# Group loop of a graph rotation: a pass now inverts, moves and applies its own group, the V chain stands ahead of the loop, and SyncE loads the edges

## What is computed

```python
x = x + gnn(xn, edge_weight, src, dst) + mix(xn)
x = x + ffn(layernorm(x))

# gnn: a product of plane rotations, in the order of the edges; mat starts as the identity (256x256)
ri, rj = mat[i], mat[j]
mat = mat.at[i].set(c * ri - s * rj)
mat = mat.at[j].set(s * ri + c * rj)
# ... return x @ mat.T
# mix: sm = softmax(keys, over the rows); lam = sm.T @ value; bn = batch norm of lam; return query @ bn
# ffn: 8 experts, the two best of each row, gelu between two products
```

## Time and profile before

| | |
|---|---|
| median of three runs | 741.78 us |
| the profiled execution's own time | 743.47 us |
| its span (first to last instruction) | 741.6 us |
| busy TensorE, VectorE, ScalarE, GpSimd | 87%, 64%, 60%, 53% |

### The profile page before, as it was taken

The page is one execution under the profiler, slowest core; times in us unless marked ns, Lnnn a source line. Parts: engine busy times, 40 slices in busy tenths (PEclk is TensorE's granted clock), DMA queues, the critical chain, the costliest instruction groups (busy, mean ns, idle before and its releaser), DMA issues.

```text
span 741.6 us, 18150 instructions
## 1 busy us (share of the span) xinstructions
PE 646.9 (87%) x4083; PEld 552.9 (75%) x4084; DVE 477.8 (64%) x1883; ACT 443.4 (60%) x1226; POOL 394.1 (53%) x541
## 2 busy tenths in 40 slices
PE   6789899754498999229999999899989999999996
PEld 5467667522487777129998999899979999999996
DVE  4996666699867688624454444444457777777775
ACT  6776566477033399616665666566656666666663
POOL 7203877145532267733776776432246665656654
PEclk7889999955599999759999999999999999999999
DMA  7830012246410267622443333322223333333332
GB/s 202 263 88 10 21 31 26 43 127 219 138 34 2 60 197 242 220 89 88 144 132 126 118 121 122 93 65 69 63 70 103 107 99 107 105 101 95 106 95 70
DMA packets 60591, 78.10 MB, mean 105 GB/s; under 512 B 15688, under 2 KB 49350, under 8 KB 60288
## 3 DMA queue, kind: packets, MB, share of 16 engines
q1 hardware_dynamic: 44989, 41.67, 20.5%
q0 software_dynamic: 14976, 35.38, 14.5%
q10 hardware_dynamic: 576, 0.54, 0.2%
HBM read 47.53 MB, written 31.53 MB: 107 GB/s over the span
## 4 chain that ended last, share of the span: by engine, by line
PE 66%; DVE 12%; issue 7%; DMA 5%; POOL 5%; ACT 2%; SPq 1%; DVEq 1%; POOLq 0%; ACTq 0%
PE banks L2679 21%; PE banks L2689 20%; PE banks L2305 6%; PE banks L2631 5%; PE banks L2284 4%; POOL send_d L900 3%; PE banks L2670 3%; DMA R<-send_d 2%; DVE R L1743 1%; DMA out_dram<-R,dest_now 1%; DMA R<-in_x_dram 1%; PE banks L2295 1%; DVE R L1758 1%; DVE R L1322 1%; PE banks L2523 1%
## 5 line engine op out<-in xcount | busy, mean ns | idle before, releaser
L2679 PE MATMUL banks<-R 128*128 128x128 f32 x1696 | 209.0, 277 | 2.6 <-ACT R L1271 2.6
L2679 PEld LDWEIGHTS banks<-R 128*128 128x128 f32 x1696 | 199.7, 193 | 3.2 <-ACT R L1271 3.1
L2689 PE MATMUL banks<-R 128*128 x848 | 200.4, 379 | 0.0
L1284 ACT ACTIVATE R<-banks,b1c 128x128 f32<-128x128 f32 x424 | 142.9, 364 | 51.4 <-PE banks L2679 51.3
L2689 PEld LDWEIGHTS banks<-R 128*128 128x128 f32 x848 | 153.1, 190 | 16.4
L1271 ACT ACTIVATE R<-banks,bet_c,gam_c 128x128 f32<-128x128 f32 x212 | 85.4, 453 | 115.0 <-PE banks L2670 112.5
L2192 DVE COPY R<-R 128x1024 f32 x106 | 74.5, 703 | 77.9 <-PE banks L2679 61.8
L900 POOL DMA_INDIRECT send_d<-R,slot_all x98 | 98.4, 1004 | 44.5 <-issue 39.1
L913 POOL DMA_INDIRECT first_d<-R,dest_now x54 | 61.2, 1134 | 91.4 <-DVE R L2197 77.7
L922 POOL DMA_INDIRECT R<-first_d,get_now x52 | 54.0, 1038 | 49.1 <-DVE get_now L2174 46.0
L913 POOL DMA_INDIRECT out_dram<-R,dest_now x52 | 63.7, 1225 | 29.6 <-issue 26.3
(11 more groups left out here) (561 smaller groups left out, 960.3 us busy)
## 6 DMA issues: line engine op xcount, KB each, us to landing
R<-send_d SPq DMA_DIRECT2D x106, 131.0 KB
...
send_d<-R,slot_all POOLq DMA_INDIRECT x98
...
```

Source lines behind the costliest of these rows:

```text
L1284: last = nc.scalar.activation(hT[b][:, c, :], bank[2 + 2 * b + c // 2][:, (c % 2) * P:(c % 2 + 1) * P], ACT.Gelu, bias=b1c[:, bass.ds(e, 1 ...
L2679: last = mm(bank[2 + 2 * b + c // 2][:, (c % 2) * P:(c % 2 + 1) * P], w1c[b][:, kb, c * P:(c + 1) * P], xmT[b][:, kb * P:(kb + 1) * P], st ...
L2689: last = mm(bank[6 + b][:, 0:D], hT[b][:, c, :], w2s[:, bass.ds(e, 1), c, :].rearrange("p a h -> p (a h)"), start=(c == 0), stop=(c == H / ...
```

## The change

It has four parts. (1) A pass of the loop runs the six levels first and then transforms and applies its own group; no empty group, no application behind the loop. (2) The V chain, the router's sums and the split of the added row stand ahead of the loop, parts of them among the placing of the events. (3) Behind the loop Mrot is first added to the base (L1972 before) and the sum is turned; one product (L2592 before), its copy and one sum over the matrix are gone, and the row sums come with the copy out of the PSUM bank. (4) SyncE loads the edges behind `load_x(1)`, `load_x(2)` waits for nothing, and on VectorE `count_rest` stands ahead of the first `mix_step`.

The loads, GpSimd's list, and VectorE's first steps:

```diff
-                if i == 2:
-                    sp.wait_ge(S["edges"], 96)
                 sp.dma_start(x_all[:, c:c + 8, :], xg_src[:, c:c + 8, :]).then_inc(S[f"xld{i}"], 16)
...
+            load_x(1)
+            for dstt, s in ((hi_raw.bitcast(I32), src), (hj_raw.bitcast(I32), dst), (h_theta, edge_weight)):
+                sp.dma_start(dstt, s[0:HP * HL].rearrange("(p l) -> p l", p=HP)).then_inc(S["edges_h"], 16)
+            for dstt, s in ((i_raw, src), (j_raw, dst), (theta, edge_weight)):
+                for into, out_of in zip(parts_of(dstt), parts_of(s.rearrange("(p l) -> p l", p=EP))):
+                    sp.dma_start(into, out_of).then_inc(S["edges"], 16)
+            for i in range(2, FULL // 8):
                 load_x(i)
...
                 link(nc.gpsimd.memset(padd[:, c:c + 1], -1.0))
-            for dstt, s in ((hi_raw.bitcast(I32), src), (hj_raw.bitcast(I32), dst), (h_theta, edge_weight)):
-                nc.gpsimd.dma_start(dstt, s[0:HP * HL].rearrange("(p l) -> p l", p=HP)).then_inc(S["edges_h"], 16)
-            for dstt, s in ((i_raw, src), (j_raw, dst), (theta, edge_weight)):
...
-            pool.wait_ge(S["ngroups"], 1)
-            n = pool.value_load(n_groups_i[0:1, 0:1], min_val=1, max_val=4 * NE)
-            with loop(pool, 0, n) as k:
...
-            pool.wait_ge(S["recs_in"], n * (16 * G) + 3 * 16 * G)
+            pool.wait_ge(S["recs_in"], 3 * 16 * G)
...
+            pool.wait_ge(S["ngroups"], 1)
+            n = pool.value_load(n_groups_i[0:1, 0:1], min_val=1, max_val=4 * NE)
+            with loop(pool, 0, n) as k:
+                fields(k + 2)
+                gather_steps(k + 3)
+
+
+            pool.wait_ge(S["recs_in"], n * (16 * G) + 3 * 16 * G)
...
             row_stats("xld1", 8, 16).then_inc(S["xstats_ok"], 1)
+            count_rest()
             mix_step(0)
             scales(3)
-            count_rest()
             count_head()
```

ScalarE's copies and the batch norm ahead of the loop, and VectorE's part of it (`tl` and `own` make VectorE wait for the instruction itself):

```diff
+                if c == 9:
+                    turned_back(PT, P_TURNED)
                 if c == 24:
                     pair_angles(0)
             pair_angles(1)
+            turned_back(wqT, WQ_TURNED)
+            table_of(ACT.Sqrt)
+            act.wait_ge(S["lamstats_ok"], 1)
+            nc.scalar.activation(small[:, 4:6], mvl[:, :, 1], ACT.Sqrt, bias=eps).then_inc(S["act"], 1)
+            act.wait_ge(S["lamstats_ok"], 2)
+            for kb in range(KB):
+                last = nc.scalar.activation(bn[:, kb, :], lam[:, kb, :], ACT.Identity, bias=small[:, 10 + kb:11 + kb], scale=small[:, 8 + kb:9 + kb])
+            last.then_inc(S["bn_ok"], 1)
 
...
+                dve.wait_ge(S["pe"], VALUES)
+                nc.vector.memset(addrow[:, D + NX:DC], 0.0)
+                for kb in range(KB):
+                    last = STT(lam[:, kb, :], bank[5][:, kb * D:(kb + 1) * D], rsum[:, kb:kb + 1], bvB[:, :], ALU.mult, ALU.add)
+                tl(last)
+                for kb in range(KB):
+                    last = nc.vector.bn_stats(lamstats[:, kb, :], lam[:, kb, :])
+                tl(last)
+                for kb in range(KB):
+                    last = nc.vector.bn_aggr(mvl[:, kb, :], lamstats[:, kb, :])
+                last.then_inc(S["lamstats_ok"], 1)
...
+                dve.wait_ge(S["edge_pe"], U_A)
+                tl(own_keys(0))
+                tl(own_values(0))
+                tl(own_sums(0))
+                dve.wait_ge(S["act"], LAM_ROOTS)
+                nc.vector.reciprocal(bn_scale, small[:, 4:6])
+                dve.wait_ge(S["edge_pe"], U_B)
+                tl(own_keys(1))
+                TT(bn_scale, bn_scale, bng_c[:, :], ALU.mult)
+                tl(own_values(1))
+                STT(bn_shift, mvl[:, :, 0], -1.0, bn_scale, ALU.mult, ALU.mult)
+                tl(own_sums(1))
...
             dve.wait_ge(S["empty_group"], 1)
+            dve.wait_ge(S["pe"], ROW_ADDED)
+            nc.vector.tensor_copy(add_c[:, :], bank[6][:, AT_ADD:AT_ADD + KB])
+            TT(brB[:, :], bank[6][:, AT_SUMS + NX:AT_SUMS + 2 * NX], brB[:, :], ALU.add)
+            nc.vector.tensor_copy(addrow[:, 0:D], bank[6][:, 0:D])
+            for kb in range(KB):
+                last = STT(comb[:, kb, D + NX:AVG], bank[6][:, AT_SUMS:AT_SUMS + NX], -1.0 / D, wrg[:, kb, :], ALU.mult, ALU.add)
+            last.then_inc(S["setup_own"], 1)
             first_guess(0)
+            dve.wait_ge(S["setup_own"], 1)
+            own(nc.vector.tensor_reduce(addrow[:, AVG:AVG + 1], addrow[:, 0:D], AX_X, ALU.add))
+            TS(addrow[:, AVG:AVG + 1], addrow[:, AVG:AVG + 1], 1.0 / D, None, ALU.mult)
             find_last(0)
+            dve.wait_ge(S["pe"], LOGIT_ADDED)
+            nc.vector.tensor_copy(addrow[:, D:D + NX], bank[6][:, AT_LOGITS:AT_LOGITS + NX]).then_inc(S["addrow_ok"], 1)
```

VectorE's loop, and what stands behind it:

```diff
                 other_rows(k)
+                factor(k, 1)
                 find_hits(k1, (0, 1))
-                factor(k, 1)
-                apply_m(k, 0)
+                factor(k, 2)
                 find_hits(k1, HALVES[1])
-                factor(k, 2)
+                factor(k, 3)
                 find_latest(k1)
-                apply_m(k, 1)
-                factor(k, 3)
+                factor(k, 4)
+                rows_read(k)
+                factor(k, 5)
+                kept(k)
                 mark_latest(k1)
-                apply_m(k, 2)
-                factor(k, 4)
                 own_reads(k1)
                 other_part(k1)
                 build_L(k1)
-                factor(k, 5)
-                rows_read(k)
+                apply_m(k, 0)
+                first_guess(k1)
                 find_last(k1)
...
-
+            own(last)
+            own(TT(Mrot[:, :, D - 1], Mrot[:, :, D - 1], flush[:, 1, :], ALU.add))
             dve.wait_ge(S["recs_in"], n * (16 * G) + 3 * 16 * G)
             dve.wait_ge(S["flds_ready"], n + 2)
             dve.wait_ge(S["Y_ready"], n + 1)
-            dve.wait_ge(S["pe"], 7)
+            dve.wait_ge(S["pe"], BASE)
             TT(turned0, bank[1].rearrange("p (a b) -> p a b", a=KB), Mrot[:, :, :], ALU.add).then_inc(S["combT_ok"], 1)
             dve.wait_ge(S["comb_pe"], 1)
-            dve.wait_ge(S["comb_moved"], 1)
-            TT(comb[:, :, 0:D], comb[:, :, 0:D], TB.rearrange("p (a b) -> p a b", a=KB), ALU.add).then_inc(S["comb_dve"], 1)
+            for kb in range(KB):
+                last = STT(comb[:, kb, 0:D], TB[:, kb * D:(kb + 1) * D], 1.0, zrow[:, 0:D], ALU.mult, ALU.add, accum_out=csum[:, kb:kb + 1])
+            last.then_inc(S["comb_dve"], 1)
             dve.wait_ge(S["comb_dve"], 1)
-            nc.vector.tensor_reduce(csum[:, :], comb[:, :, 0:D], AX_X, ALU.add).then_inc(S["comb_dve"], 1)
-            dve.wait_ge(S["comb_dve"], 2)
```

TensorE:

```diff
                     spread_rows(g + 2)
+            values()
             pe.wait_ge(S["pair_dve"], FULL_ROWS)
             mm(bank[6][:, 0:KB], ones[:, :], bad[:, 5:7], start=True, stop=True).then_inc(S["edge_pe"], 1)
...
-            for _ in range(14):
+            router_sums()
+            for _ in range(6):
                 mm(bank[6][:, 0:P], ident[:, :], ident[:, :], start=True, stop=True)
+            added_row()
...
+            added_logits()
 
             n = pe.value_load(n_groups_i[0:1, 0:1], min_val=1, max_val=4 * NE)
 
             with loop(pe, 0, n) as k:
-                transform(k)
                 residual(k, 0)
                 spread_targets(k + 1)
                 better(k, 0)
-                apply_v(k, 0)
                 residual(k, 1)
-                apply_m(k, 0)
                 better(k, 1)
                 residual(k, 2)
-                apply_v(k, 1)
                 better(k, 2)
-                apply_m(k, 1)
                 residual(k, 3)
-                apply_v(k, 2)
                 better(k, 3)
-                apply_m(k, 2)
                 residual(k, 4)
                 better(k, 4)
                 residual(k, 5)
                 count_writes(k)
+                better(k, 5)
+                transform(k)
+                apply_v(k, 0)
+                apply_m(k, 0)
                 count_later(k + 1)
                 turn_L(k + 1)
-                better(k, 5)
-            transform(n)
-            pe.wait_ge(S["wload"], 16 * 10)
-            pe.wait_ge(S["pn_ok"], 1)
...
+                apply_m(k, 2)
+            base_rows(0)
+            base_rows(1).then_inc(S["pe"], 1)
+            for _ in range(3):
+                mm(bank[0][:, 0:P], ident[:, :], ident[:, :], start=True, stop=True)
+            pe.wait_ge(S["combT_ok"], 1)
             for a in range(KB):
                 for b in range(KB):
-                    last = tr(TB[:, b * D + a * P:b * D + (a + 1) * P], Mrot[:, a, b * P:(b + 1) * P], ident[:, :])
+                    last = tr(TB[:, b * D + a * P:b * D + (a + 1) * P], turned0[:, a, b * P:(b + 1) * P], ident[:, :])
             last.then_inc(S["comb_pe"], 1)
-            pe.wait_ge(S["combT_ok"], 1)
             for ib in range(KB):
                 for a in range(KB):
```

(2 more changed lines are left out.)

241 lines of the change are left out of this document (96 added, 145 removed).

## The result

The changed kernel took 737.4 us (median of 20 runs, 731.64 to 744.54), the kernel before 742.55 in runs beside it (20 runs, 738.78 to 745.75). The ratio is 0.9934, 95% interval 0.9912 to 0.9955: 3.3 to 6.5 us faster, where 11.2 were forecast. Every ratio in this document is to the kernel before in runs beside it on the same chip, and leaves out runs more than 1.5 per cent above the fastest of their kernel (here 743.48 and 744.54).

A forecast was written before the change was run, and what follows sets the result against it. Part three was taken as a chain of short steps, TensorE busy 34.34 of 39.00 us, its empty-group work waste. Terms -3.8 + 0.5 - 2.4 - 1.85 - 3.65 = -11.2 us gave 730.6 us on the median, range 727 to 733.5 (0.66).

The forecast's parts named there:

- A: Part one, loads and first steps: load_x(1) lands earlier and the weighted-sum products start sooner and run shorter, -3.8 us.
- B: Part two and the start of the loop, up to the first residual: added and removed work sum to +0.5 us.
- Rival 2: TensorE enters the levels at half clock after fewer identity products, some 3 us more, 733.6 us; chance 0.12.
- The prediction's own sign against itself: The forecast is wrong if PEclk, the granted clock, is below 1 in the loop.
- C: The six levels: without the 128x256 products between residual and better, 14.8 us against 17.16, -2.4 us.
- D: From transform to the last application: V chain's products and sums gone, 11.75 us against 13.6, -1.85 us.
- E: Behind the last application: first sum comes 4.45 us later against 8.1, -3.65 us.
- late gather: Within E, VectorE's sum behind the loop waits for GpSimd's last gathered records; without it 0.9 us less.
- Behind 247.00 nothing is changed, and its start moves as a whole: From the first sum on, experts included, the kernel only starts earlier and takes as long as before: 0 us.
- Rival 3: Half the gain is given back later, by a wait of the routing for GpSimd or a load: 736 us; chance 0.06.
- Rival 4: Granted clock falls to half in the whole loop without the removed products: +15.3 us, +4.1 net, 745.9 us; chance 0.04.

The follow-up runs named there:

- loads_only: The kernel before with part (4) alone (edges on SyncE behind load_x(1), no wait in load_x(2), count_rest earlier): 739.82 us, ratio 0.9978.
- fill_pool: The changed kernel with identity products ahead of the loop, at its entrance and in the levels' waits, and GpSimd's loop ahead of the split again: 738.23 us, ratio 0.9931.
- fill_early: The changed kernel with 8 and 3 more identity products in TensorE's two waits around the product of the composites: ratio 0.9913 to the kernel before.
- ident14: The changed kernel with 14 identity products in place of 6 ahead of the added row: ratio 1.0033 to the kernel before.
- loop_only: The changed kernel with part (4), the loads, undone: 740.32 us, ratio 0.9961 to the kernel before.

## Why the prediction was wrong

The mechanisms were named rightly, and two sizes and one sentence were not.

- **A, mis-sized (-3.8 forecast, -2.7 by the means of the traces, -1.8 by the medians of `loads_only`'s pair, whose ratios show none).** The order of the loads works as put: the 4 us wait is gone in all four traces. The step that failed is the base. The profiled execution had a late `load_x(1)` and a granted clock of 0.71 in the products; I priced both as if they were the rule. In the second trace of before the load comes 1.5 us sooner (16.87, still with a wait of 3.38) and the products take 3.69 us. They end at 36.81 there, at 40.41 in the profiled execution and at 36.00 after the change: most of the 3.8 was in the one trace.
- **B, mis-sized, and its place is where the clock is lost (+0.5 forecast, +2.2 measured).** Rival 2, given 0.12, is what happens in two of four traces: 15.1 us to the first residual in place of 12.8, a loss of 2.2 and not the 3 forecast. Even the better two are 1.1 us behind before. The router's sums and the added row (L2531, L2533, L2539 and L2543) were put at 2 us at full clock and 3.7 at half; they took 3.6 us in the first trace (0.89 from 194.54 and 2.74 from 197.45) and 5.0 in the second. The prediction's own sign against itself, a granted clock below 1 in the loop, came true (0.50 from 204 to 206).
- **C, right in its mechanism (-2.4 forecast, -1.9 measured).** A level without foreign products takes 2.13 us as read. The missing 0.5 is more than covered by the clock in the first two levels: at a full clock (14.15 us, `fill_pool`) the term would have been -3.0.
- **D and E, right: -5.5 forecast, -5.6 measured.** In the first trace 11.86 us for D (11.75 forecast) and 4.15 for E (4.45), with the late gather where it was said to be, 0.65 us in place of 0.9.
- **"Behind 247.00 nothing is changed, and its start moves as a whole" is the step that failed most: +2.1 us net.** The experts take 2.7 us longer. Some 1.5 of it is VectorE's standstill, behind which TensorE waits 1.4 to 1.8 us and which the 64 memsets remove: a changed instruction list can change how an untouched loop behind it is entered. The rest lies in a second place: in three of four traces of the changed kernel and one of three of before the clock falls once near the middle of the experts, behind waits of 0.5 and 1.3 us that both kernels have. After the change it is 0.83 in 460 to 470, and before 1.00 in 470 to 480:

```profile
460.00:470.00 10.00, 8.17 (x47) 7.33 (x46) 3.29 (x12) 4.21 (x13) 2.45 (x3) 0.83 0.24 76
```
```profile
470.00:480.00 10.00, 8.11 (x55) 7.06 (x54) 3.46 (x12) 4.72 (x14) 2.95 (x3) 1.00 0.25 77
```

  Over all 20 traces this fall is in 7 of the 16 with the changed loop and in 2 of the 4 with the loop of before: nothing says that the change makes it likelier, and its part of the difference (2 us in 3 of 4 traces against 1 of 3, some 0.8) is the luck of the draw. Rival 3 (half given back later, 0.06, "nothing in a row speaks for it") came nearest to the measured time, by a mechanism that it didn't name.
- **Rival 4 (the clock at half in the whole loop)** did not come about in the four traces of the changed kernel, but in kernels near this one it did in part (`fill_early`, 16 us at 0.50; `ident14`, behind its standstill; `loop_only`, levels of 19.33 us). The four are of runs of 734.3 to 738.2 us, while the kernel's runs reach 744.5, so how often it falls so deep is not known. Against it I had put that the levels are mostly TensorE, beside 0.9 of 2.13 us, which is not even half. The windows of `fill_early` show that a busy TensorE is no protection: a busy share of 0.97 stood beside 0.50. What decides how deep the clock falls, and so what exactly the fillers do, stays open: the seven traces with fillers in the levels or at their entrance never had it (14.15 to 15.7 us), but one or two traces for each kernel are not enough, and no edit brought the fall about on purpose. The Trainium skill (TensorE: Matmul & The Clock Gate, Part 1) describes a clock that follows how busy TensorE has been and oscillates where it idles briefly between groups of products. The clock of the first trace after (1.00, 0.50, 1.00 and 0.60 from 186, 190, 194 and 198) agrees with it in kind; the 16 us at half with 0.97 busy are not told by it.

Worked out together: of the 6.0 us between forecast and median gain, 1.1 lie in A, 1.8 in B and the way to it, 0.5 in C and 2.1 behind the first sum, less 0.1 in D and E: 5.4; the remaining 0.6 is the difference between the traces' mean and the medians.
